# Fewer waits of VectorE on its own semaphore in the attention stage of a transformer block on eight cores

## The chip, the cores and the metric

The kernel runs on all 8 cores of one Trainium2 chip. Each core works on its own 2 of the 16 sequences and sends nothing to the others. The metric is the device time in microseconds (us) of the slowest core; lower is better. The profile is of one execution, on the slowest of its cores (core 3).

## The reference

One pre-norm block: windowed causal attention, then a feed-forward part with ternary weights and 8-bit activations. x is 16 x 2048 x 1024, float32, with 16 heads of 64 and a window of 128.

```python
qkv = layernorm(x) @ w_qkv                 # q, k, v: 16 heads of 64
scores = q k^T / 8, kept where (j <= i) & (j > i - 128)
x = x + (softmax(scores) v) @ w_out
h = gelu(bitlinear(layernorm(x), W1, b1))  # 1024 -> 4096
x = x + bitlinear(h, W2, b2)               # 4096 -> 1024
# bitlinear: weights rounded to -1, 0, 1 times mean|W|,
# activations rounded to 8 bits by the token's absolute maximum
```

## The kernel before, in words

A core has 4096 tokens, cut into 32 tiles of 128 tokens. The program has two stages. The attention stage goes over the 32 tiles, writes each tile's x + attention to a scratch tensor in HBM, and on the side prepares the ternary weights. The feed-forward stage then goes over the 32 tiles again. The change touches only the attention stage.

The order of the work is written out by hand. Each call of `op(engine, fn, waits, nosync=...)` appends one instruction to a list; at the end `mk` (line 1257) walks over the list once per engine. Three rules of it matter:

- Every VectorE (DVE), ScalarE (ACT) and GpSimd instruction raises its engine's own semaphore by one: sV for VectorE, sA for ScalarE. TensorE (PE) raises sP at the end of a group.
- The semaphores named in `waits` are waited for with one `wait_ge` each (line 1268), unless the engine has already waited for as high a value.
- Unless the instruction has `nosync=True`, one more `wait_ge` is put before it (line 1273), on the engine's own semaphore at the number of instructions issued so far. The engine then waits until its previous instruction has completed. Below this is called the own wait.

```python
for (s, val) in waits:
    if val > 0 and lastw.get(s.name, 0) < val:
        eng.wait_ge(s.h, val)
        lastw[s.name] = val
...
if zs is not None and zi > 0 and not ns:
    eng.wait_ge(zs.h, zi)
inst = fn(eng)
```

In the attention stage a tile t is worked on with parts of tile t+1 between. On VectorE, in order:

- `a_ln1_stats(t+1)`: sum over the tile's x (L493), then three instructions on one column (L496, L499, L502). L493 needs the transfer of x, which is issued after L798 of the tile before.
- For each of four groups g of four heads: `a_sm_max`, two maxima over half a group's scores each (L656, L661), which need TensorE's scores; ScalarE's exponentials (L683) follow; `a_sm_norm`, a reciprocal of two row sums (L700), two scalings of 128x256 (L713), another reciprocal (L708), two more scalings. The scaled probabilities are transposed by TensorE (L734), copied by ScalarE (L745), and multiplied with v (L763).
- `a_ln2_fin(t-1)`: L821, L825, L828 on one column.
- `a_ln1_apply(t+1)`: L518 on one column; ScalarE then writes the normalized x (L523), TensorE transposes it (L534), ScalarE copies it (L540).
- Weight preparation, eight tasks to a tile. Tiles 0 to 15 do absolute sums (L402, L409); tiles 16 to 31 round a piece of weights (L421, L426, L430), which TensorE transposes (L443) and VectorE copies out (L455 or L464). I call them sum tiles and rounding tiles.
- From the start of TensorE's q projection of tile t+1 (L556 into psA): the last group's scaling, the k copy (L574), the copy of the attention output (L776), the residual add (`a_res`, L798), and the v copy (L580). Here TensorE does the q, k and v projections (L556 into psA, psB, psC) and the output projection (L787).

TensorE takes the work in program order: scores of group 0 and 1; scores of group 2, transposes and product of group 0; scores of group 3, those of group 1; the transposes of x; those of group 2; then the q projection.

Of the kernel before, what the change touches and what calls it, by code (L numbers as in the profile page):

```python
# [43 lines left out]
def _build(nt, mode="full", cut=None):  # L44
# [106 lines left out]
    with ExitStack() as ctx:  # L151
# [6 lines left out]
        sP = _Sem("sP"); sV = _Sem("sV"); sA = _Sem("sA"); sG = _Sem("sG")  # L158
        dX = _Sem("dX"); dS = _Sem("dS"); dL = _Sem("dL"); dO = _Sem("dO")
# [11 lines left out]
        def op(ek, fn, waits=(), inc=None, amt=1, is_dma=False,  # L171
               nosync=False):
            if fn is not None and not is_dma and ek in _ES:
                inc = _ES[ek]
                amt = 1
            OPS.append((ek, [w for w in waits if w is not None and w[1] > 0],
                        fn, inc, amt, is_dma, nosync))
            if inc is not None:
                inc.n += amt
                return inc.n  # L180
            return None
# [6 lines left out]
        ms = {}  # L188
# [35 lines left out]
        def _memset(ap_, val):  # L224
# [21 lines left out]
                waits=[(dY, _w)], inc=sA)  # L246
        _b = dma("act", bbf_d[0:HF].rearrange("(p k) -> p k", p=128), bstage_bf,
                 dY, waits=[(sA, _a)])
        dma("act", b1bf, bbf_d[0:HF].rearrange("(a k) -> a k", a=1), dY,
            waits=[(dY, _b)])  # L250
        _w = dma("act", bstage[:, 0:8], b2_d.rearrange("(p k) -> p k", p=128),
                 dY, waits=[(dY, _b)])
        _a = op("act", lambda e: e.activation(out=bstage_bf[:, 0:8],
                                              in_=bstage[:, 0:8], func=AF.Copy),
                waits=[(dY, _w)], inc=sA)
# [3 lines left out]
            waits=[(dY, _b)])  # L259
        ms["bias_ld"] = dY.n  # L260

        xin_ld = {}
# [39 lines left out]
        if mode == "S":  # L302
            v = op("dve", lambda e: e.tensor_copy(out=outbuf, in_=wqkv_sb[:, 0:D]),
                   waits=[(sV, wc_v), (sA, wc_a), (dX, dX.n), (dY, ms["bias_ld"]),
                          (dC, ms["consts_ld"])])
# [180 lines left out]
        def a_ln1_stats(t):  # L486
            par = t % 2
            cl = cells[t % 2]
            va = op("act", lambda e, x=xin[par], c=cl: e.activation(
                out=outbuf, in_=x, func=AF.Square,  # L490
                accum_out=c[:, CEL_SSQ:CEL_SSQ + 1]),
                waits=[(dX, xin_ld[t])], inc=sA)
            op("dve", lambda e, x=xin[par], c=cl: e.tensor_reduce(  # L493
                out=c[:, CEL_SUM:CEL_SUM + 1], in_=x, axis=AX.X, op=ALU.add),
                waits=[(dX, xin_ld[t])])
            op("dve", lambda e, c=cl: e.tensor_scalar(  # L496
                out=c[:, CEL_M:CEL_M + 1], in0=c[:, CEL_SUM:CEL_SUM + 1],
                scalar1=1.0 / D, scalar2=None, op0=ALU.mult))
            op("dve", lambda e, c=cl: e.tensor_tensor(  # L499
                out=c[:, CEL_MSQ:CEL_MSQ + 1], in0=c[:, CEL_M:CEL_M + 1],  # L500
                in1=c[:, CEL_M:CEL_M + 1], op=ALU.mult))
            v = op("dve", lambda e, c=cl: e.scalar_tensor_tensor(  # L502
                out=c[:, CEL_VAR:CEL_VAR + 1], in0=c[:, CEL_SSQ:CEL_SSQ + 1],
                scalar=1.0 / D, in1=c[:, CEL_MSQ:CEL_MSQ + 1],
                op0=ALU.mult, op1=ALU.subtract), waits=[(sA, va)], inc=sV)
            op("act", lambda e, c=cl: e.activation(
                out=c[:, CEL_LNV:CEL_LNV + 1], in_=c[:, CEL_VAR:CEL_VAR + 1],
                func=AF.Ln, bias=c_eps),
                waits=[(sV, v), (sV, ms["memset"])])
            va = op("act", lambda e, c=cl: e.activation(  # L510
                out=c[:, CEL_RSTD:CEL_RSTD + 1], in_=c[:, CEL_LNV:CEL_LNV + 1],
                func=AF.Exp, scale=-0.5), inc=sA)
            ms[("rstd", t)] = va
# [139 lines left out]
        def a_sm_max(t, g):  # L653
            cl = cells[t % 2]
            psX = psA if g % 2 == 0 else psB
            v0 = op("dve", lambda e, p=psX, c=cl, g_=g: e.tensor_reduce(  # L656
                out=c[:, CEL_NMX + 4 * g_:CEL_NMX + 4 * g_ + 2],
                in_=p[:, 0:512].rearrange("p (h k) -> p h k", h=2),
                axis=AX.X, op=ALU.max, negate=True),
                waits=[(sP, ms[("sc_h0", t, g)])], inc=sV)  # L660
            v = op("dve", lambda e, p=psX, c=cl, g_=g: e.tensor_reduce(  # L661
                out=c[:, CEL_NMX + 4 * g_ + 2:CEL_NMX + 4 * g_ + 4],
                in_=p[:, 512:1024].rearrange("p (h k) -> p h k", h=2),
                axis=AX.X, op=ALU.max, negate=True),
                waits=[(sP, ms[("scores", t, g)])], inc=sV, nosync=True)
            ms[("nmx0", t, g)] = v0
            ms[("nmx", t, g)] = v
# [29 lines left out]
        def a_sm_norm(t, g):  # L697
            cl = cells[t % 2]
            ev = ms[("expv", t, g)]
            r0 = op("dve", lambda e, c=cl, g_=g: e.reciprocal(  # L700
                out=c[:, CEL_RCP + 4 * g_:CEL_RCP + 4 * g_ + 2],
                in_=c[:, CEL_SUMS + 4 * g_:CEL_SUMS + 4 * g_ + 2]),
                waits=[(sA, ev[1])], inc=sV)
            rc = r0
            v2 = None
            for hh in range(4):
                if hh == 2:
                    rc = op("dve", lambda e, c=cl, g_=g: e.reciprocal(  # L708
                        out=c[:, CEL_RCP + 4 * g_ + 2:CEL_RCP + 4 * g_ + 4],
                        in_=c[:, CEL_SUMS + 4 * g_ + 2:  # L710
                               CEL_SUMS + 4 * g_ + 4]),
                        waits=[(sA, ev[3])], inc=sV)
                v2 = op("dve", lambda e, c=cl, g_=g, hh_=hh: e.tensor_scalar(  # L713
                    out=probsn[g_ % 2][:, hh_ * 256:(hh_ + 1) * 256],
                    in0=probs[g_ % 2][:, hh_ * 256:(hh_ + 1) * 256],
                    scalar1=c[:, CEL_RCP + 4 * g_ + hh_:
                              CEL_RCP + 4 * g_ + hh_ + 1],
                    scalar2=None, op0=ALU.mult),
                    waits=[(sV, rc)], inc=sV, nosync=(hh in (1, 3)))
                if hh == 1:  # L720
                    ms[("pn0", t, g)] = v2
            ms[("pn", t, g)] = v2
# [73 lines left out]
        def a_res(t):  # L796
            par = t % 2
            v = op("dve", lambda e, x=xin[par], o=x1buf[par]: e.tensor_tensor(  # L798
                out=o, in0=psC, in1=x, op=ALU.add),
                waits=[(sP, ms[("outproj", t)]), (dS, spill_ms.get(t - 2, 0))],  # L800
                inc=sV)
            ms[("res", t)] = v
            psum_free["C"] = (sV, v)
            spill_ms[t] = dma("syncq", x1_d[t * T:(t + 1) * T, :], x1buf[par],
                              dS, waits=[(sV, v)])
# [41 lines left out]
        for t in range(nt):  # L847
# [60 lines left out]
            if t + 2 < nt:  # L908
                xin_ld[t + 2] = dma(
                    "syncq", xin[t % 2], xc[(t + 2) * T:(t + 3) * T, :],  # L910
                    dX, waits=[(sV, ms[("res", t)]), (sA, ms[("xln", t)])])
# [6 lines left out]
        for ek in ("pe", "dve", "act", "pool", "syncq"):  # L918
            waits = [(ENG_SEM[o], a_end[o]) for o in ENG_SEM if o != ek]
# [5 lines left out]
        for j in range(4):  # L925
# [3 lines left out]
                waits=([(dB[0], dB[0].n), (dB[1], dB[1].n)] if j < 2 else [])))  # L929
# [33 lines left out]
        for t in range(min(3, nt)):  # L963
            x1_ld[t] = dma("syncq", x1s(t), x1_d[t * T:(t + 1) * T, :],
                           dL, waits=[(dS, dS.n)])
# [368 lines left out]
```

How the kernel before makes its waits and increments, by code:

```python
        def run(eng):  # L1260
            lastw = {}
            zi = 0
            for (k, waits, fn, inc, amt, is_dma, ns) in OPS:
                if k != ek:
                    continue
                for (s, val) in waits:
                    if val > 0 and lastw.get(s.name, 0) < val:
                        eng.wait_ge(s.h, val)
                        lastw[s.name] = val
                if fn is None:
                    continue
                if zs is not None and zi > 0 and not ns:
                    eng.wait_ge(zs.h, zi)
                inst = fn(eng)
                if zs is not None and not is_dma:
                    zi += 1
                if inc is not None:
                    inst.then_inc(inc.h, amt)
```

## Time and profile before

| | us |
|---|---|
| median of 2 runs | 3181.88 (3154.82 and 3208.95) |
| the profiled execution, its time | 3148.21 |
| its span on core 3 | 3146.6 |
| the spans of all cores | 3135.2 to 3146.6 |
| VectorE busy in that span | 2002.7 |
| TensorE busy in that span | 2248.0 |

The time of an execution is 1.6 us more than the span of its slowest core; what lies outside the span is small. All eight cores have the same work, and their spans lie within 12 us.

### The profile page before, as it was taken

What the parts mean: (1) busy time and instruction counts of PE and PEld (TensorE: products, weight loads), DVE (VectorE), ACT (ScalarE), POOL (GpSimd) and SP (SyncE); (2) the same over time, 40 slices, a digit from 0 to 9 for tenths busy, and PEclk for the clock granted to TensorE, in tenths of its full rate; (3) what the DMA queues carried; (4) which work ended last, traced back from release to release, by engine and by line L of the source; (5) the groups of instructions that cost most, each with busy time, mean ns of one, the idle gap of its engine ahead of it and who ended that gap; (6) DMA issues with size and microseconds to landing.
All of it is one profiled execution on the core that took longest, in us unless ns stands there. A gap on an engine that the chain in (4) does not pass through costs nothing.

```text
span 3146.6 us, 41087 instructions; the slowest of 8 cores (3135.2 to 3146.6 us)
## 1 busy us (share of the span) xinstructions
PE 2248.0 (71%) x13196; PEld 1077.6 (34%) x13196; DVE 2002.7 (64%) x3711; ACT 1066.6 (34%) x2064; POOL 17.8 (1%) x36
## 2 busy tenths in 40 slices
PE   0376676676666666666666588888888888888887
PEld 0133333333333333333333233333333333333332
DVE  1245545545546566666666577778777778777775
ACT  1345545544534344444343122222222222222221
POOL 0000000000000000000000000000000000000000
PEclk9977786787777777777776899999999999999998
DMA  4222122222211111122322300000000000000000
GB/s 156 91 76 73 61 74 68 64 71 68 72 51 59 58 61 61 64 81 74 88 74 68 137 27 28 27 15 27 27 27 27 28 14 28 27 27 27 27 15 20
DMA packets 94344, 170.69 MB, mean 54 GB/s; under 512 B 41138, under 2 KB 41394, under 8 KB 93619
## 3 DMA queue, kind: packets, MB, share of 16 engines
q1 hardware_dynamic: 84480, 125.86, 13.0%
q10 hardware_dynamic: 5044, 25.44, 2.3%
q0 software_dynamic: 4608, 16.78, 1.3%
q8 instruction: 108, 1.77, 0.2%
q14 instruction: 104, 0.85, 0.1%
HBM read 126.09 MB, written 41.95 MB: 53 GB/s over the span
## 4 chain that ended last, share of the span: by engine, by line
PE 55%; DVE 17%; ACT 11%; issue 9%; DMA 6%; DVEq 1%; ACTq 0%; SPq 0%; POOLq 0%
PE psC L1191 15%; PE psA L983 8%; PE psB L983 7%; PE psA L556 5%; ACT hqT L1174 4%; PE psC L787 4%; PE psB L556 4%; DMA xin<-xc 3%; DVE probs L713 2%; DVE cells L661 2%; DVE wqch L430 2%; ACT probsT L745 2%; DMA wstgB<-wqkv 2%; PE psC L556 1%; ACT qT L609 1%
## 5 line engine op out<-in xcount | busy, mean ns | idle before, releaser
L1191 PE MATMUL psC<-W2qT,hqT 128*128 128x512 bf16 x2048 | 489.6, 391 | 121.7 <-ACT hqT L1174 121.7
L1191 PEld LDWEIGHTS psC<-W2qT,hqT 128*128 128x128 bf16 x2048 | 192.3, 99 | 368.8 <-issue 173.7
L983 PE MATMUL psA<-W1qT,xqT 128*128 128x512 bf16 x1024 | 249.0, 387 | 0.0
L983 PE MATMUL psB<-W1qT,xqT 128*128 128x512 bf16 x1024 | 243.2, 380 | 0.0
L1007 DVE TENSOR_REDUCE cells<-h_sb 128x1 f32<-128x1024 f32 x128 | 150.2, 1212 | 143.2 <-ACT h_sb L1000 143.2
L763 PE MATMUL psC<-probsT,v_hist 128*64 128x128 bf16 x1024 | 75.1, 289 | 204.3 <-ACT probsT L745 204.3
L955 DVE TENSOR_TENSOR tib<-t1a,tfb 128x1024 f32<-128x1024 f32 x160 | 196.0, 1225 | 17.0 <-DVE tfb L954 0.5
L574 DVE CAST k_sb<-psB 128x1024 bf16<-128x1024 f32 x32 | 39.2, 1224 | 233.6 <-PE psB L556 233.6
L1174 ACT ACTIVATE hqT<-psD 128x1024 bf16<-128x1024 bf16 x64 | 65.5, 1024 | 330.2 <-PE psD L1164 330.2
L1174 ACT ACTIVATE hqT<-psF 128x1024 bf16<-128x1024 bf16 x64 | 65.5, 1024 | 325.8 <-PE psF L1164 325.8
L556 PE MATMUL psA<-wqkv_sb,xlnT 128*128 128x512 bf16 x512 | 174.3, 516 | 1.4 <-ACT xlnT L540 1.4
L957 DVE SCALAR_TENSOR_TENSOR hq<-tfb,tib 128x1024 bf16<-128x1024 f32 x128 | 156.8, 1225 | 13.7 <-DVE tib L955 0.5
L631 PE MATMUL psA<-kT_hist,qT 64*128 64x128 bf16 x512 | 63.4, 260 | 129.2 <-ACT probs L683 128.0
L713 DVE TENSOR_SCALAR probs<-probs,cells 128x256 bf16<-128x256 bf16 x512 | 123.4, 283 | 46.1 <-DVE cells L700 23.4
L556 PE MATMUL psC<-wqkv_sb,xlnT 128*128 128x512 bf16 x512 | 115.6, 379 | 50.3 <-DVE x1b L798 50.3
L798 DVE TENSOR_TENSOR x1b<-psC,xin 128x1024 f32<-128x1024 f32 x32 | 39.2, 1224 | 150.0 <-PE psC L787 144.4
L983 PEld LDWEIGHTS psA<-W1qT,xqT 128*128 128x128 bf16 x1024 | 90.8, 99 | 124.2 <-issue 35.8
L983 PEld LDWEIGHTS psB<-W1qT,xqT 128*128 128x128 bf16 x1024 | 89.7, 98 | 119.7 <-issue 29.0
L763 PEld LDWEIGHTS psC<-probsT,v_hist 128*64 128x64 bf16 x1024 | 50.6, 146 | 231.8 <-issue 231.8
L683 ACT ACTIVATE probs<-psA,cells 128x256 bf16<-128x256 f32 x256 | 118.0, 473 | 15.9 <-DVE cells L656 12.8
L954 DVE CAST tfb<-tib 128x1024 f32<-128x1024 int32 x160 | 111.0, 694 | 16.8 <-DVE tib L953 0.5
L953 DVE CAST tib<-t1a 128x1024 int32<-128x1024 f32 x160 | 111.0, 694 | 16.5
(159 smaller groups left out, 3733.0 us busy)
## 6 DMA issues: line engine op xcount, KB each, us to landing
wstage<-w SPq DMA_DIRECT2D x256, 256.0 KB, 2.8
xin<-xc SPq DMA_DIRECT2D x32, 512.0 KB, 4.4
x1sp<-x1b SPq DMA_DIRECT2D x32, 512.0 KB, 2.9
y<-outbuf POOLq DMA_DIRECT2D x32, 512.0 KB, 4.6
x1b<-x1sp SPq DMA_DIRECT2D x22, 512.0 KB, 3.8
w2td<-w2st SPq DMA_DIRECT2D x64, 128.0 KB, 2.0
W2qT<-w2td ACTq DMA_DIRECT2D x4, 2048.0 KB, 12.3
wstgA<-wqkv ACTq DMA_DIRECT2D x8, 768.0 KB, 4.6
```

Source lines behind the costliest of these rows:

```text
L556: e.matmul(out=p[:, nn * 512:(nn + 1) * 512], lhsT=xlnT[:, cc * 128:(cc + 1) * 128], rhs=wqkv_sb[:, cc * 3 * D + g * D + nn * 512: cc * 3 ...
L683: e.activation(out=probs[g_ % 2][:, hh_ * 256:(hh_ + 1) * 256], in_=p[:, hh_ * 256:(hh_ + 1) * 256], func=AF.Exp, bias=c[:, CEL_NMX + 4 * ...
L713: v2 = op("dve", lambda e, c=cl, g_=g, hh_=hh: e.tensor_scalar(out=probsn[g_ % 2][:, hh_ * 256:(hh_ + 1) * 256], in0=probs[g_ % 2][:, hh_ ...
L763: kt_=kt, sl=slot, g_=g: e.matmul(out=psC[bp_:bp_ + 64, pp * 128:(pp + 1) * 128], lhsT=v_hist[:, sl * D + h_ * 64: sl * D + h_ * 64 + 64], ...
L787: pv = op("pe", lambda e, cc=c, nn=n: e.matmul(out=psC[:, nn * 512:(nn + 1) * 512], lhsT=attnout[:, cc * 128:(cc + 1) * 128], rhs=wout_sb[ ...
L953: op("dve", lambda e: e.tensor_copy(out=tib, in_=t1b))
L955: op("dve", lambda e: e.tensor_tensor(out=cbb, in0=t1b, in1=tfb, op=ALU.is_ge))
L957: rl = op("dve", lambda e, rr=r, d=dst_ap: e.scalar_tensor_tensor(out=d[:, rr * 1024:(rr + 1) * 1024], in0=tfb, scalar=-641.0, in1=cbb, op ...
L983: e.matmul(out=p[:, nn * 512:(nn + 1) * 512], lhsT=xqT[:, cc * 128:(cc + 1) * 128], rhs=W1qT[:, cc * HF + jj * 1024 + nn * 512: cc * HF + ...
L1007: op("dve", lambda e, jj=j, c=cl: e.tensor_reduce(out=c[:, FH + jj:FH + jj + 1], in_=h_sb[:, jj * 1024:(jj + 1) * 1024], axis=AX.X, op=ALU ...
L1174: evs = op("act", lambda e, rr_=rr, p=sp: e.activation(out=hqT[:, rr_ * 1024:(rr_ + 1) * 1024], in_=p, func=AF.Copy), waits=[(sP, pv)] + ( ...
L1191: pv = op("pe", lambda e, nn=n, kk=k: e.matmul(out=psC[:, nn * 512:(nn + 1) * 512], lhsT=hqT[:, kk * 128:(kk + 1) * 128], rhs=W2qT[:, kk * ...
```

## The change

Six `op` calls of VectorE in the attention stage get `nosync=True` (one of them already had it on two of its four instructions, and now has it on three). No instruction is added, removed or moved; the waits named in `waits` all stay. What goes is the own wait (line 1273) ahead of:

- L493, the sum over x: one in a tile
- L656, the maximum over the first half of a group: four in a tile
- L700 and L708, the two reciprocals: four each in a tile
- L713, the third of the four scalings: four in a tile. It keeps a wait for the same value of sV, since `waits` names the reciprocal just ahead of it
- L798, the residual add: one in a tile

That is 18 in a tile, and 576 in the 32 tiles.

```diff
@@ a_ln1_stats
             op("dve", lambda e, x=xin[par], c=cl: e.tensor_reduce(
                 out=c[:, CEL_SUM:CEL_SUM + 1], in_=x, axis=AX.X, op=ALU.add),
-                waits=[(dX, xin_ld[t])])
+                waits=[(dX, xin_ld[t])], nosync=True)
@@ a_sm_max
-                waits=[(sP, ms[("sc_h0", t, g)])], inc=sV)
+                waits=[(sP, ms[("sc_h0", t, g)])], inc=sV, nosync=True)
@@ a_sm_norm
-                waits=[(sA, ev[1])], inc=sV)
+                waits=[(sA, ev[1])], inc=sV, nosync=True)
...
-                        waits=[(sA, ev[3])], inc=sV)
+                        waits=[(sA, ev[3])], inc=sV, nosync=True)
...
-                    waits=[(sV, rc)], inc=sV, nosync=(hh in (1, 3)))
+                    waits=[(sV, rc)], inc=sV, nosync=(hh > 0))
@@ a_res
                 waits=[(sP, ms[("outproj", t)]), (dS, spill_ms.get(t - 2, 0))],
-                inc=sV)
+                inc=sV, nosync=True)
```

VectorE's rows in a sum tile, from the second group's maximum to the third's, before. In the brackets are the semaphores that an instruction waits for, each named once; cells are the columns of row statistics, probs the probabilities:

```order
L828 SCALAR_TENSOR_TENSOR cells_49<-cells_49 128x1 [waits sV]
L656 TENSOR_REDUCE cells_48<-psB 128x2 [waits sP,sV]
L661 TENSOR_REDUCE cells_48<-psB 128x2 [waits sP]
L700 RECIPROCAL cells_48<-cells_48 128x2 [waits sA,sV]
L713 TENSOR_SCALAR probs_73<-probs_73,cells_48 128x256 [waits sV]
L713 TENSOR_SCALAR probs_73<-probs_73,cells_48 128x256
L708 RECIPROCAL cells_48<-cells_48 128x2 [waits sA,sV]
```

The same rows with the change:

```order
L828 SCALAR_TENSOR_TENSOR cells_49<-cells_49 128x1 [waits sV]
L656 TENSOR_REDUCE cells_48<-psB 128x2 [waits sP]
L661 TENSOR_REDUCE cells_48<-psB 128x2 [waits sP]
L700 RECIPROCAL cells_48<-cells_48 128x2 [waits sA]
L713 TENSOR_SCALAR probs_73<-probs_73,cells_48 128x256 [waits sV]
L713 TENSOR_SCALAR probs_73<-probs_73,cells_48 128x256
L708 RECIPROCAL cells_48<-cells_48 128x2 [waits sA]
```

The order stays. L656, L700 and L708 no longer name sV, and wait only for TensorE or ScalarE.

## Rows read from the trace of the kernel before

**Rows 1.** The head of the page.

```profile
span 3146.6 us, 41087 instructions; the slowest of 8 cores (3135.2 to 3146.6 us)
```

**Rows 2.** Stretches: length; busy us (x instructions) of each engine; clock, DMA share, GB/s.

```profile
141.00:891.00 750.00, 522.54 (x3484) 273.67 (x3484) 379.06 (x958) 369.63 (x847) 0.00 (x0) 0.76 0.21 68
891.00:1740.00 849.00, 556.54 (x3882) 306.57 (x3880) 519.83 (x1218) 361.44 (x839) 0.00 (x0) 0.73 0.22 68
1740.00:3146.00 1406.00, 1153.88 (x5760) 490.45 (x5760) 1081.55 (x1504) 311.46 (x353) 17.62 (x32) 0.97 0.09 31
```

**Rows 3.** The chain that ended last, shares of the whole span.

```profile
PE 55%; DVE 17%; ACT 11%; issue 9%; DMA 6%; DVEq 1%; ACTq 0%; SPq 0%; POOLq 0%
```

**Rows 4.** The chain, 478.2 to 478.7 us: start, us, what (DVEq is VectorE's sequencer).

```profile
478.22 0.02 DVEq L1273
...
478.29 0.18 DVE cells L708
...
478.49 0.02 DVEq L1268
...
478.56 0.02 DVEq L1273
...
478.63 0.09 DVE probs L713
```

**Rows 5.** Timeline of VectorE in a sum tile: start, duration, line.

```profile
478.63 0.48 DVE L713 TENSOR_SCALAR probs<-probs,cells 128x256 bf16<-128x256 bf16 x2 [0.18 <-DVE cells L708]
479.21 0.69 DVE L656 TENSOR_REDUCE cells<-psA 128x2 f32<-128x512 f32 x1
479.82 0.68 DVE L661 TENSOR_REDUCE cells<-psA 128x2 f32<-128x512 f32 x1
```

**Rows 6.** Timeline of VectorE where an unsynced instruction follows a short one.

```profile
902.87 0.16 DVE L383 TENSOR_SCALAR b<-psF 128x1 f32<-128x1 f32 x1
902.98 0.48 DVE L421 TENSOR_SCALAR sgnA<-wstage,b 128x512 bf16<-128x512 f32 x1
```

**Rows 7.** The chain around a residual add (L798).

```profile
460.47 3.58 PE psC L787 x16
...
464.21 0.02 DVEq L1273
...
464.28 1.24 DVE x1b L798
```

**Rows 8.** Timeline of ScalarE and TensorE in the sum tile that begins at 471.88 us.

```profile
474.42 0.20 ACT L510 ACTIVATE cells<-cells 128x1 f32<-128x1 f32 x1
...
474.83 0.47 ACT L683 ACTIVATE probs<-psA,cells 128x256 bf16<-128x256 f32 x1 [0.21 <-DVE cells L656]
...
478.50 0.61 PE L643 MATMUL psA<-masks,identb 128*128 128x256 bf16 x2
...
483.82 1.19 PE L734 MATMUL psF<-identb,probs 128*128 128x128 bf16 x8
...
484.80 1.24 ACT L523 ACTIVATE xln<-xin,cells 128x1024 bf16<-128x1024 f32 x1 [1.70 <-DVE cells L518]
...
485.95 1.00 ACT L745 ACTIVATE probsT<-psF 128x1024 bf16<-128x1024 bf16 x1
...
487.67 1.03 PE L534 MATMUL psD<-identb,xln 128*128 128x128 bf16 x8
...
489.91 0.59 PE L734 MATMUL psF<-identb,probs 128*128 128x128 bf16 x4 [0.34 <-DVE probs L713]
```

**Rows 9.** Timeline of TensorE at the end of a rounding tile's softmax part.

```profile
1030.07 0.58 PE L443 MATMUL psD<-identb,wqch 128*128 128x128 bf16 x4 [0.34 <-DVE wqch L430]
```

**Rows 10.** Who waited for whom, VectorE: us in total, times, longest us.

```profile
DVE cells L493 <- DMA xin<-xc: 8.7, 9, 1.6
```

**Rows 11.** Costliest groups, q and v projections: busy us, mean ns | idle before.

```profile
L556 PE MATMUL psA<-wqkv_sb,xlnT 128*128 128x512 bf16 x512 | 174.3, 516 | 1.4 <-ACT xlnT L540 1.4
L556 PE MATMUL psC<-wqkv_sb,xlnT 128*128 128x512 bf16 x512 | 115.6, 379 | 50.3 <-DVE x1b L798 50.3
```

## The prediction

> **What bounds the kernel now.** The head of the page comes first: 3146.6 us on the slowest of eight like cores [rows 1]. Then the stretches [rows 2]. The attention stage is the first two rows: 750 us for the 16 sum tiles, about 46.9 a tile, and 849 us for the 16 rounding tiles, about 53.1 a tile. The feed-forward stage, 1406 us, holds none of the changed instructions. TensorE's granted clock is 0.76 and 0.73 in the attention rows: it changes between its two levels (1.2 and 2.4 GHz) within a tile. No engine is busy all the time there; VectorE is at 379 of 750 and 520 of 849. The chain gives TensorE 55% and VectorE 17% [rows 3], but over the whole span. So I read one tile in the timeline. It falls in two halves. From L493 to the start of the q projection (about 20 us in a sum tile, more in a rounding tile) VectorE has hardly a gap and TensorE waits for it. From there to the next L493 TensorE is busy and VectorE waits for it. The change can pay only in the first half, and at L798 in the second.
>
> **One own wait.** The chain shows it as the sequencer's step at L1273, which comes only once the scaling has ended; L708 starts 0.07 behind that step (478.22, 478.29) [rows 4]. In the timeline L656 starts 0.10 after the end of the pair ahead of it (478.63 + 0.48 = 479.11, start 479.21), while L661, which has no own wait, starts 0.08 before the end of L656 (479.21 + 0.69 = 479.90, start 479.82) [rows 5]. An own wait therefore costs 0.10 + 0.08, about 0.19 us with rounding. Behind a short instruction of one column it is less: L421 starts 0.05 before the end of L383 [rows 6], so 0.16. That price goes to the L656 of groups 1 and 3 (behind L828 and L518) and in sum tiles to two L700 (behind L409).
>
> At the third scaling two waits stand in a row for one value, L1268 and L1273, 0.07 us apart [rows 4]. The first stays, so only 0.07 goes. At L798 TensorE ends at 464.05 (460.47 + 3.58), and the last of three waits behind it is the one removed (464.21, start 464.28) [rows 7]: again 0.07. The bounds: 0 from a wait that was satisfied long before, 0.19 from a full own wait.
>
> The Trainium skill speaks against all this: its page "VectorE: DVE Perf Modes", section "The DRAIN you can't avoid", says that eight copies took 13.88 us with a semaphore after each and also with one after the last, and that "the semaphore costs nothing extra here". By that rule the sum is 0. The rows above disagree, by 0.19 us a wait; the rule is about raising the semaphore, and here the engine also waits for it.
>
> **What is on the path in a tile.** Up to the end of group 2's scaling there are on VectorE: L493, four L656, three L700, three L708, three third scalings. Group 3's scaling comes behind the start of the q projection, where VectorE has several us to spare; its three cost and save nothing. Without L493 the rest is 10 x 0.19 + 3 x 0.07 = 2.1 us, less 0.06 to 0.12 for the short ones: 2.0.
>
> Not all of it goes through, since the other engines come up. In the sum tile at 471.88 [rows 5, 8]:
>
> - ScalarE's first exponential waits for L656, 0.21 us after L510 ended (474.62, start 474.83). Behind L510 it needs about 0.10 of its own, so it can come only 0.11 earlier, however early L656 is. The scores of group 2 wait for these exponentials, so they come 0.11 earlier too. They end at 479.11 (478.50 + 0.61), and L661 starts at 479.82: slack 0.71. A wait on TensorE needs about 0.11. So L661 can come 0.71 - 0.11 + 0.11 = 0.71 earlier, where VectorE by itself would be 1.0 earlier. Here 0.3 us are lost. I take the same slack for all tiles.
> - Group 1's transposes stand behind the scores of group 3, and these behind group 0's transposes, ScalarE's copy and the product: a chain that moved 0.11. They end at 485.01 (483.82 + 1.19), and would end at 484.90. ScalarE's copy at 485.95 was held by its own queue (L523 to 486.04, which waited for L518). With L518 1.1 us earlier the transposes set it: about 484.98, so 0.97 earlier. The product and the transposes of x follow, which end at 488.70 (487.67 + 1.03) - 0.97 = 487.73.
> - Group 2's transposes come next, 0.59 each half. TensorE had waited 0.34 before the second half, at 489.91. VectorE would let it start about 1.7 earlier (0.71 + 0.16 + 0.19 + 0.07 for group 1, 0.16 for L656, 0.16 + 0.19 + 0.07 for group 2). TensorE is ready at 487.73 + 0.59 = 488.32, which is 1.59 earlier. So the q projection starts 1.6 earlier.
>
> In a rounding tile VectorE also feeds the transposes of the weights, so TensorE is brought back to VectorE's time on the way and at the end ([rows 9]: 0.34 us of waiting for VectorE just before the q projection). Only the 0.3 at the first L661 is lost: 0.71 + 0.45 + 0.16 + 0.45, 1.8 us.
>
> **The sum.**
>
> - 16 sum tiles x 1.6 = 25.6
> - 16 rounding tiles x 1.8 = 28.8
> - L798: 31 x 0.07 = 2.2. TensorE waits for it before the v projection [rows 11], and the transfer of x is issued behind it.
> - L493: 14 rounding tiles x 0.19 = 2.7, and perhaps 0.7 in the sum tiles. In nine tiles of both kinds the transfer of x ends the wait [rows 10], and there it saves nothing; in the other sum tiles I count a tenth of a microsecond.
>
> That makes 60 us: 3148.2 - 60 = 3088 us, 1.9% less. The time is against the profiled execution's own 3148.21; the two runs shown are 0.2% and 1.9% above it, and their median 1.1%.
>
> Late next are L661 of group 2, which will wait 0.3 us for TensorE in each tile, and in the sum tiles TensorE's own queue ahead of group 2's transposes (0.1 us of VectorE's gain is left unused there, and 0.3 before).
>
> **Bounds.** If each own wait saved only the 0.10 of the gap, and none of the overlap, the sum would be near 35 us (10 x 0.10 + 3 x 0.07 = 1.2 a tile, 31 tiles: 37), so 3111. If all of VectorE's 2.0 went through in each tile, with 0.19 for each L493: 32 x 2.0 + 6 + 2 = 72, so 3076. The value between them goes by the rows, which show the overlap in pairs of the same kind. The unknown is TensorE's clock: the q projection's matmuls take 516 ns on average against 379 in psC [rows 11], since the clock comes back within it. That is 16 x 0.137 = 2.2 us a tile, and where in it the clock comes back depends on when the tile began. A shift of 0.4 us in its mean is 13 us over the stage, either way.
>
> **Rivals.**
>
> - *All of it goes through.* For it: VectorE has no gaps in the first half. Against: the 0.71 us of slack at L661, less than the 1.0 saved by then. 3076 us, 2.3% less.
> - *TensorE and ScalarE take more than I count.* At the lower clock they are nearly as late as VectorE in the sum tiles; ScalarE's exponentials, copies and x run one behind another. For it: [rows 8], where TensorE had waited for VectorE only 0.34 us in the end. Half the gain goes through: 3148 - 36 = 3112.
> - *Nothing is saved*, because VectorE's next instruction starts at the same time anyway. Against: [rows 4, 5]. 3148 us. The skill's section named above gives this time.
> - *Slower, by the clock.* If the shifted halves left TensorE at 1.2 GHz through the k projection too, its 16 matmuls would take twice as long: the 16 of L787, at the higher level, take 3.58 us [rows 7]; with some of the time hidden, I put 3.3 us more a tile. In all 31 tiles that is 102, less 60: 3190 us. It decides from 60 / 3.3 = 18 tiles on. Against: before the rise TensorE does the same work as now, and it waits less.
>
> **How the numbers follow.** Chances: forecast 0.58, all of it 0.15, half of it 0.17, nothing 0.06, slower 0.04. The forecast's own range is 3073 to 3103, from the clock's 13 us and 0.1% between runs. The range for 8 in 10 reaches down past the full sum by the clock's luck, to 3060, and up past the half to 3122. 2% (about what a measurement can tell from no change here) is 3085 us. The forecast's case lies below it 4 times in 10 (0.23), the full sum always (0.15): 0.38 faster. Slower by over 2% would need 3211, past my worst case: 0.02. The rest, 0.60, is within 2%.
>
> **What would show it.** Right: VectorE's L656, L700 and L708 start 0.05 to 0.08 before the end of the instruction ahead; L713 behind L708 starts 0.10 after it, where it was 0.17, and behind L700 still 0.17; L661 of group 2 shows a new wait for TensorE (L643) of 0.2 to 0.4 us in most tiles; the sum tiles' stretch of 16 falls from 750 to about 723, the rounding tiles' from 849 to about 815; the feed-forward stage stays at 1406. Wrong: gaps of 0.10 that stay; the q projection starting as late after L493 as before; a mean of L556 into psA far from 516 ns.

## The result and the profile after

The median of the changed kernel is 3092.14 us (11 runs), that of the kernel before 3148.61 (10 runs). The ratio is 0.9806, with a 95% interval from 0.9781 to 0.9831: 1.9% less, about 61 us. The profiled execution took 3082.89 us. The forecast was 3088. In four of the eleven executions cores of one die or of both were granted a lower clock and the time was longer; the median counts them, the ratio doesn't.

The head of the page, two of its costliest groups and its chain of waits, for the changed kernel (core 4, the slowest):

```profile
span 3081.3 us, 40334 instructions; the slowest of 8 cores (3072.8 to 3081.3 us)
...
PE 58%; ACT 13%; DVE 13%; issue 8%; DMA 6%; DVEq 0%; ACTq 0%; SPq 0%; POOLq 0%
...
L556 PE MATMUL psA<-wqkv_sb,xlnT 128*128 128x512 bf16 x481 | 163.7, 514 | 10.0 <-DVE cells L708 5.0
...
L713 DVE TENSOR_SCALAR probs<-probs,cells 128x256 bf16<-128x256 bf16 x512 | 123.7, 283 | 37.7 <-DVE cells L700 23.2
```

In the chain [rows 3] VectorE's share fell from 17 to 13%, its sequencer's from 1 to 0, and ScalarE's rose from 11 to 13%. One thing needs care: the q projection has 481 of its 512 matmuls in the records, one short in each of 31 tiles [rows 11]. The missing one is the first, so the matmul row seems to start 0.4 us late. Below I take the start of the q projection from its first weight load, which is there.

The stretches, cut at the first L493 of tiles 1 and 17 and just behind the last L798. [rows 2] can't be set beside them as it stands: its first cut is 2.6 us behind that L493, its last 6.6 us behind the end of L798. So first the kernel before, cut alike:

```profile
138.44:891.94 753.50, 523.48 (x3494) 274.22 (x3494) 381.58 (x963) 370.22 (x849) 0.00 (x0) 0.76 0.21 68
891.94:1734.00 842.06, 555.60 (x3874) 306.02 (x3871) 518.50 (x1214) 358.85 (x834) 0.00 (x0) 0.73 0.22 67
```

and the changed kernel:

```profile
135.00:855.50 720.50, 510.11 (x3469) 275.91 (x3502) 368.50 (x963) 370.41 (x848) 0.00 (x0) 0.77 0.23 71
855.50:1667.00 811.50, 550.25 (x3831) 308.17 (x3862) 502.38 (x1214) 358.74 (x834) 0.00 (x0) 0.73 0.24 70
1667.00:3081.00 1414.00, 1145.41 (x5648) 490.76 (x5760) 1082.46 (x1508) 313.35 (x359) 17.84 (x32) 0.96 0.10 31
```

Sum tiles: 720.5 where there were 753.5, 33.0 less. Rounding tiles: 811.5 where there were 842.1, 30.6 less. The feed-forward stage is what it was within 2 us (1414 and 1412).

VectorE in the softmax half of a sum tile of the changed kernel (start, duration, line):

```profile
500.92 0.16 DVE L502 SCALAR_TENSOR_TENSOR cells<-cells 128x1 f32<-128x1 f32 x1
501.03 0.69 DVE L656 TENSOR_REDUCE cells<-psA 128x2 f32<-128x512 f32 x1
...
503.46 0.68 DVE L661 TENSOR_REDUCE cells<-psB 128x2 f32<-128x512 f32 x1
504.06 0.15 DVE L700 RECIPROCAL cells<-cells 128x2 f32<-128x2 f32 x1
504.39 0.48 DVE L713 TENSOR_SCALAR probs<-probs,cells 128x256 bf16<-128x256 bf16 x2 [0.17 <-DVE cells L700]
504.79 0.16 DVE L708 RECIPROCAL cells<-cells 128x2 f32<-128x2 f32 x1
505.05 0.48 DVE L713 TENSOR_SCALAR probs<-probs,cells 128x256 bf16<-128x256 bf16 x2
505.45 0.68 DVE L656 TENSOR_REDUCE cells<-psA 128x2 f32<-128x512 f32 x1
506.30 0.69 DVE L661 TENSOR_REDUCE cells<-psA 128x2 f32<-128x512 f32 x1 [0.16 <-PE psA L643]
```

Read the gaps by adding start and duration and looking at the next start. L700 now starts 0.08 before the end of L661; L708 and L656 start 0.08 before the end of L713 (it was 0.10 after, [rows 5]). L713 behind L708 starts 0.10 after it (0.17 before), and behind L700, whose two waits were left, still 0.18. L656 behind the one-column L502 starts 0.05 before its end. And the last row has a new wait: L661 of group 2 for the scores.

The views of L661, what ended the idle time before it; first the kernel before, then the changed one (us in total, times):

```profile
  PE psA L643: 0.3, 1
```

```profile
  PE psA L643: 4.7, 25
```

In 25 of 32 tiles VectorE now waits for group 2's scores, 0.19 us on average. Without a wait L661 starts 0.08 before the end of L656, so a tile that waits loses 0.27.

The chain at a residual add of the changed kernel:

```profile
488.06 3.42 PE psC L787 x15
...
491.50 0.02 DVEq L1268
...
491.57 0.02 DVEq L1268
...
491.63 1.24 DVE x1b L798
```

Of three sequencer steps two are left, and L798 starts 0.15 behind TensorE (488.06 + 3.42 = 491.48), where it was 0.23 in [rows 7]; by the medians over all tiles it is 0.18 and 0.25.

### The profile page after: what moved, and what is told of

Its sections match the earlier page's. It is cut to its first block, busy times and chain, and to the rows that moved or that the text cites. A ratio compares the mean times of both kernels' runs of the same rounds, so it can differ in the third digit from the quotient of the medians.

```text
span 3081.3 us, 40334 instructions; the slowest of 8 cores (3072.8 to 3081.3 us)
## 1 busy us (share of the span) xinstructions
PE 2220.0 (72%) x13019; PEld 1081.5 (35%) x13196; DVE 1973.7 (64%) x3711; ACT 1066.2 (35%) x2064; POOL 18.0 (1%) x36
## 4 chain that ended last, share of the span: by engine, by line
PE 58%; ACT 13%; DVE 13%; issue 8%; DMA 6%; DVEq 0%; ACTq 0%; SPq 0%; POOLq 0%
PE psC L1191 15%; PE psA L983 8%; PE psB L983 7%; PE psA L556 5%; ACT hqT L1174 4%; PE psB L556 4%; PE psC L787 4%; DMA xin<-xc 3%; ACT probsT L745 3%; DVE wqch L430 2%; ACT probs L683 2%; DMA wstgB<-wqkv 2%; PE psC L556 2%; ACT qT L609 1%; PE psA L975 1%
## 5 line engine op out<-in xcount | busy, mean ns | idle before, releaser
L1191 PE MATMUL psC<-W2qT,hqT 128*128 128x512 bf16 x1984 | 471.4, 384 | 128.0 <-ACT hqT L1174 125.4
L983 PE MATMUL psA<-W1qT,xqT 128*128 128x512 bf16 x992 | 257.7, 403 | 3.3 <-issue 2.5
L556 PE MATMUL psA<-wqkv_sb,xlnT 128*128 128x512 bf16 x481 | 163.7, 514 | 10.0 <-DVE cells L708 5.0
L713 DVE TENSOR_SCALAR probs<-probs,cells 128x256 bf16<-128x256 bf16 x512 | 123.7, 283 | 37.7 <-DVE cells L700 23.2
L798 DVE TENSOR_TENSOR x1b<-psC,xin 128x1024 f32<-128x1024 f32 x32 | 39.2, 1225 | 149.6 <-PE psC L787 149.6
```

Of the source, the lines that this page charges most:

```text
L556: e.matmul(out=p[:, nn * 512:(nn + 1) * 512], lhsT=xlnT[:, cc * 128:(cc + 1) * 128], rhs=wqkv_sb[:, cc * 3 * D + g * D + nn * 512: cc * 3 ...
L983: e.matmul(out=p[:, nn * 512:(nn + 1) * 512], lhsT=xqT[:, cc * 128:(cc + 1) * 128], rhs=W1qT[:, cc * HF + jj * 1024 + nn * 512: cc * HF + ...
L1191: pv = op("pe", lambda e, nn=n, kk=k: e.matmul(out=psC[:, nn * 512:(nn + 1) * 512], lhsT=hqT[:, kk * 128:(kk + 1) * 128], rhs=W2qT[:, kk * ...
```

## The experiments

The whole times of most kernels move by one or two per cent, and so each kernel was also read tile by tile. The table gives means over 14 sum tiles (2 to 15) and 14 rounding tiles (17 to 30), worked out from the timelines of the three engines on the slowest core of each profiled execution: from the v copy (L580) to the start of the q projection (the softmax half), from there to ScalarE's copy of q (L566), and the whole tile from v copy to v copy. The ratio is to the kernel before. The rest of a tile is 18.2 to 18.7 us in all of them.

| kernel | ratio (95%) | sum: softmax half | q | tile | rounding: softmax half | q | tile |
|---|---|---|---|---|---|---|---|
| before | 1 | 22.42 | 5.75 | 46.68 | 29.59 | 5.48 | 53.37 |
| changed | 0.9806 (0.9781 to 0.9831) | 20.53 | 5.63 | 44.48 | 27.40 | 5.82 | 51.42 |
| x1_max_only | 0.9900 (0.9876 to 0.9924) | 21.82 | 5.69 | 46.02 | 28.90 | 5.18 | 52.50 |
| x2_norm_only | 0.9827 (0.9801 to 0.9853) | 21.11 | 5.53 | 45.29 | 28.13 | 5.06 | 51.52 |
| x3_ends_only | 0.9963 (0.9942 to 0.9984) | 22.32 | 5.56 | 46.33 | 29.35 | 5.35 | 52.91 |
| x4_more_own_waits | 1.0166 (1.0139 to 1.0194) | 24.40 | 5.55 | 48.46 | 31.58 | 5.07 | 54.92 |
| z1_edits_in_sum_tiles | 0.9771 (0.9745 to 0.9797) | 20.46 | 5.66 | 44.45 | 28.10 | 5.19 | 51.49 |
| y2_sums_behind_maxima | 0.9789 (0.9750 to 0.9828) | 19.70 | 6.41 | 44.43 | 27.42 | 5.61 | 51.23 |
| y3_four_more_waits | 0.9781 (0.9739 to 0.9824) | 20.24 | 5.89 | 44.46 | 27.16 | 5.84 | 51.21 |
| y4_both | 0.9714 (0.9682 to 0.9746) | 19.12 | 5.78 | 43.23 | 27.05 | 5.94 | 51.19 |
| w1_fill_weight_loads | 0.9704 (0.9686 to 0.9723) | 19.06 | 5.62 | 43.00 | 27.15 | 6.07 | 51.43 |
| w2_fill_transposes | 0.9588 (0.9570 to 0.9606) | 18.90 | 4.15 | 41.49 | 26.99 | 5.49 | 50.68 |
| w3_fill_first_gap | 0.9706 (0.9685 to 0.9727) | 19.26 | 5.77 | 43.47 | 27.20 | 5.48 | 50.89 |

### The price of one wait: the edits apart, and more waits

Only the edit at L656:

```diff
@@ a_sm_max, first half
-                waits=[(sP, ms[("sc_h0", t, g)])], inc=sV)
+                waits=[(sP, ms[("sc_h0", t, g)])], inc=sV, nosync=True)
```

> Of the six edits only the one at L656 is made. Theory A (an own wait costs 0.19 us, 0.16 behind a one-column instruction, and VectorE's time passes through until L661 of group 2 meets the scores): 0.19 + 0.16 + 0.19 + 0.16 = 0.70 us a tile, no new wait at L661 of group 2 (its slack falls from 0.71 to about 0.17 above the least possible), 22 us less than before, about 3126. Theory B (only the gap of 0.10 counts): 4 x 0.10, 13 us. Theory C (the semaphore costs nothing and the gain came from a luckier clock): 0 us.

Measured: the softmax half is 0.60 us shorter in sum tiles and 0.69 in rounding tiles (0.72 and 0.62 by the medians of the eight cores), where theory A had 0.70 and B 0.40. The time fell by 1.0%, about 31 us by the ratio and 28 by the medians; the rest of it is in the q projection. Two parts of the 0.70 were priced wrongly, and cancel: the first L656 stands behind L502, 0.16 us long, and starts 0.05 before its end, so it is 0.16 and not 0.19; the last stands behind L518, which also has one column but takes 0.21 us, and starts 0.08 before its end, so it is 0.19 and not 0.16.

Only the edits at L700, L708 and the third L713:

```diff
@@ a_sm_norm
-                waits=[(sA, ev[1])], inc=sV)
+                waits=[(sA, ev[1])], inc=sV, nosync=True)
...
-                        waits=[(sA, ev[3])], inc=sV)
+                        waits=[(sA, ev[3])], inc=sV, nosync=True)
...
-                    waits=[(sV, rc)], inc=sV, nosync=(hh in (1, 3)))
+                    waits=[(sV, rc)], inc=sV, nosync=(hh > 0))
```

> Only the edits at L700, L708 and the third L713 are made. Theory A: three groups on the path, 0.45 us each in rounding tiles and a little less in sum tiles, 1.3 us a tile, 42 us less than before, about 3106, and no new wait at L661 of group 2. Theory B: 3 x (0.10 + 0.10 + 0.07) = 0.8 us a tile, 26 us. Theory C: 0. If A holds, this run and the one with L656 alone add up to 64, while the full change should show about 54 for the same waits, since only together do they meet the new wait at L661.

Measured: 1.31 and 1.46 us less in the softmax half, against 1.29 and 1.35 by theory A and 0.8 by B. The time fell by 1.7%, 54 us by the ratio and 51 by the medians, more than the 42 expected; the q projection became 0.2 and 0.4 us shorter as well.

Only the two at the ends:

```diff
@@ a_ln1_stats
-                waits=[(dX, xin_ld[t])])
+                waits=[(dX, xin_ld[t])], nosync=True)
@@ a_res
-                inc=sV)
+                inc=sV, nosync=True)
```

> Only the edits at L493 and L798 are made. Theory A: 0.07 us at L798 in 31 tiles and 0.19 at L493 where the transfer of x is already there: 4 to 6 us less than before, about 3143. If the full change lived from an earlier transfer of x or an earlier v projection, this run would show 15 us or more.

Measured: 0.10 and 0.24 us less in the half that holds L493, and 0.37% of the time, where 5 us were expected and 12 came by the ratio, 9 by the medians. Neither an earlier transfer nor an earlier v projection carries the change.

The other way round, with own waits added to the kernel before:

```diff
@@ a_sm_max, second half
-                waits=[(sP, ms[("scores", t, g)])], inc=sV, nosync=True)
+                waits=[(sP, ms[("scores", t, g)])], inc=sV)
@@ a_sm_norm, the scalings
-                    waits=[(sV, rc)], inc=sV, nosync=(hh in (1, 3)))
+                    waits=[(sV, rc)], inc=sV, nosync=False)
```

> The kernel before with own waits added where it had none: at L661 (four in a tile) and at the second and fourth L713 (eight in a tile, six of them before the q projection). Theory A: 10 x 0.19 = 1.9 us a tile, all of it on the path since VectorE is what the others wait for, 61 us more than before, about 3209. Theory B: 10 x 0.10, 32 us more, 3180. Theory C: no change. The gaps in the timeline should be 0.10 at each added wait in place of the overlap of 0.08.

Measured: the softmax half is 1.98 us longer in sum tiles and 1.99 in rounding tiles, for 10 waits on the path: 0.20 us each. The timeline of this kernel shows it at L661, which starts 0.11 after the end of L656 where the kernel before has it 0.08 ahead of the end:

```profile
484.62 0.69 DVE L656 TENSOR_REDUCE cells<-psA 128x2 f32<-128x512 f32 x1
485.41 0.69 DVE L661 TENSOR_REDUCE cells<-psA 128x2 f32<-128x512 f32 x1
```

The time rose by 1.66%, 52 us, and not by 61. The softmax halves account for 64; the q projection took 0.2 to 0.4 us less a tile, which gives 10 of it back.

So theory A holds for the softmax half in these kernels, and B and C are out. What no theory of mine had is the column of the q projection: it changes in every kernel, by up to 0.4 us a tile, though nothing touches it. And the parts add up to 3.1% by their ratios, where the whole gives 1.9%.

### Where the missing per cent is

The new wait at L661 explains only some of it. The parts shorten the softmax half by 0.60 + 1.31 + 0.10 = 2.01 us in sum tiles, the whole by 1.89; in rounding tiles by 0.69 + 1.46 + 0.24 = 2.39, the whole by 2.19. That is 5 us over 32 tiles. (The medians of the eight cores put nearly all of it in the sum tiles: 2.17 and 1.86 there, 2.20 and 2.16 in the rounding tiles.) More is in the q projection of the rounding tiles: 0.34 us longer than before with the whole change, and 0.13 to 0.42 shorter with each part. By their whole tiles the parts come to 2.40 and 3.18 us, the whole change to 2.20 and 1.95: 23 us over 32 tiles, 0.7%. The rest of the 1.2% is not in the tiles, and the intervals of the ratios, 0.2 to 0.3% to either side, are wide enough for it. The next kernel takes the gain at L656 and L493 away again, in the rounding tiles alone.

```diff
@@ the changed kernel
-                waits=[(dX, xin_ld[t])], nosync=True)
+                waits=[(dX, xin_ld[t])], nosync=(t <= 16))
...
-                waits=[(sP, ms[("sc_h0", t, g)])], inc=sV, nosync=True)
+                waits=[(sP, ms[("sc_h0", t, g)])], inc=sV, nosync=(t < 16))
```

> The changed kernel, but in the rounding tiles L493 and L656 have their own waits again (the other edits stay everywhere). It tests where 26 us of the parts went, since the three parts alone gave 27, 51 and 9 us and together 61. Theory K (the clock): in the rounding tiles of the changed kernel the q projection takes 5.8 us from its start to ScalarE's copy of q, against 5.1 to 5.4 in the parts, since every tile has the same length of 51.2 us and meets the clock's return at the same point. Here the tile is 0.7 us longer in the first half and at L493, and the q projection falls back to about 5.2: the two cancel, and the time stays that of the changed kernel, 3087 within 5. Theory L (the parts overlap because of the new wait at L661): the q projection stays at 5.8, and the time is 11 us above the changed kernel's, 3098.

Measured: theory K. The softmax half of the rounding tiles is 0.70 us longer than in the changed kernel, the q projection 0.63 shorter, and the tile is the same within 0.1. The ratio is 0.9771, and its interval overlaps the changed kernel's: it isn't slower, and undoing a part of the change cost nothing. The median is 3082.50, where theory K had 3087 within 5 and theory L 3098. How this looks in two neighbouring tiles: the first weight load of the q projection (PEld) and ScalarE's copy that ends it (start, duration), for the changed kernel

```profile
1192.63 0.26 PEld L556 LDWEIGHTS psA<-wqkv_sb,xlnT 128*128 128x128 bf16 x2
1243.80 0.26 PEld L556 LDWEIGHTS psA<-wqkv_sb,xlnT 128*128 128x128 bf16 x2
```

```profile
1198.52 1.02 ACT L566 ACTIVATE q_sb<-psA 128x1024 bf16<-128x1024 f32 x1 [7.83 <-PE psA L556]
1249.70 1.02 ACT L566 ACTIVATE q_sb<-psA 128x1024 bf16<-128x1024 f32 x1 [7.85 <-PE psA L556]
```

and for the one with the edits undone in these tiles:

```profile
1196.96 0.25 PEld L556 LDWEIGHTS psA<-wqkv_sb,xlnT 128*128 128x128 bf16 x2
1248.07 0.25 PEld L556 LDWEIGHTS psA<-wqkv_sb,xlnT 128*128 128x128 bf16 x2
```

```profile
1202.14 1.02 ACT L566 ACTIVATE q_sb<-psA 128x1024 bf16<-128x1024 f32 x1 [7.12 <-PE psA L556]
1253.29 1.02 ACT L566 ACTIVATE q_sb<-psA 128x1024 bf16<-128x1024 f32 x1 [7.17 <-PE psA L556]
```

5.89 and 5.90 us in the first, 5.18 and 5.22 in the second, and from one copy to the next 51.18 and 51.15. The first of each pair of q projections, cut where the granted clock (the third number from the right) rises; changed kernel, then the other:

```profile
1192.63:1196.80 4.17, 3.95 (x12) 1.63 (x12) 3.25 (x11) 0.00 (x0) 0.00 (x0) 0.50 0.24 64
1196.80:1198.52 1.72, 1.72 (x13) 0.90 (x12) 1.34 (x3) 0.00 (x0) 0.00 (x0) 1.00 0.50 148
```

```profile
1196.96:1199.70 2.74, 2.74 (x10) 1.06 (x9) 2.04 (x9) 0.00 (x0) 0.00 (x0) 0.50 0.26 88
1199.70:1202.14 2.44, 2.44 (x17) 1.26 (x16) 2.12 (x5) 0.00 (x1) 0.00 (x0) 1.00 0.35 105
```

The q projection begins at 1.2 GHz (0.50) and ends at 2.4 (1.00), with 4.17 us at the lower level in the first and 2.74 in the second. Half of the difference is 0.72 us, the difference of 5.89 and 5.18. It is so everywhere: in 356 of the 364 tiles behind the table the projection takes 3.78 us, which is its time when all of it runs at 2.4 GHz, and half of the time that it spent at the lower level, within 0.05 us. When the rise comes is not tied to the projection's start, and an earlier start only means more matmuls at the lower level.

### The cap in the sum tiles

The changed kernel, with the sum over x behind the first group's maxima in the sum tiles:

```diff
@@ the tile loop, tiles 0 to 15
-            a_ln1_stats(t + 1)
+            a_ln1_sq(t + 1)      # ScalarE's square (L489), as before
             a_scores(t, 0)
             a_sm_max(t, 0)
+            a_ln1_dve(t + 1)     # L493, L496, L499, L502
             a_sm_exp(t, 0)
...
             a_sm_exp(t, 1)
+            a_ln1_rstd(t + 1)    # L506, L510
```

> The changed kernel, but in sum tiles L493 to L502 come behind the first group's two maxima, and ScalarE's two one-column steps behind the second group's exponentials. So the first exponentials no longer stand behind the sum over x and its transfer. If the chain from L493 over the first exponentials and the scores of group 2 is what caps the gain: L661 of group 2 waits for nothing any more (0.3 us), the waits for the transfer of x in 7 of 14 sum tiles are gone (1.1 us each), the transposes of x come earlier (0.15 us); 1 us a sum tile, 17 us less than the changed kernel, 3071. If the cap lies elsewhere: only the transfer's waits go, 8 us, 3079. The clock may add or take 10 us.

Measured: both waits are all but gone. In the sum tiles VectorE waits once for scores at the second maximum (0.4 us) and once for the transfer of x (0.7), where it was 14 times and 7 times (2.8 and 6.5 us in all). VectorE's timeline in this kernel (its L672, L677 and L504 are L656, L661 and L493 of the others) begins the maxima before the v copy's record ends, and L677 of group 2 follows without a gap:

```profile
494.86 1.23 DVE L596 CAST v_hist<-psC 128x1024 bf16<-128x1024 f32 x1 [3.87 <-PE psC L572]
496.00 0.68 DVE L672 TENSOR_REDUCE cells<-psA 128x2 f32<-128x512 f32 x1
496.60 0.68 DVE L677 TENSOR_REDUCE cells<-psA 128x2 f32<-128x512 f32 x1
497.19 1.21 DVE L504 TENSOR_REDUCE cells<-xin 128x1 f32<-128x1024 f32 x1
...
502.33 0.68 DVE L672 TENSOR_REDUCE cells<-psA 128x2 f32<-128x512 f32 x1
502.93 0.68 DVE L677 TENSOR_REDUCE cells<-psA 128x2 f32<-128x512 f32 x1
```

The softmax half of the sum tiles is 0.83 us shorter, of the 1.0 expected. But the q projection is 0.78 longer, and the tile is 44.43 against 44.48. The whole gain went back to the clock; of the 17 us expected, the tiles of both kinds together leave 4. The ratio's interval (0.9750 to 0.9828) doesn't part it from the changed kernel.

More of the same kind of edit:

```diff
@@ the changed kernel: L518, the first L713, the absolute sums
-                waits=[(sA, ms[("rstd", t)])], inc=sV)
+                waits=[(sA, ms[("rstd", t)])], inc=sV, nosync=True)
...
-                    waits=[(sV, rc)], inc=sV, nosync=(hh > 0))
+                    waits=[(sV, rc)], inc=sV, nosync=True)
...
-                    out=accw[:, 4:5], in_=s, axis=AX.X, op=ALU.add,
+                    out=accw[:, k:k + 1], in_=s, axis=AX.X, op=ALU.add,
...
-                           pst["acc_rd"]], nosync=True)
+                           pst["acc_rd2"]], nosync=True)
```

> The changed kernel with more of the same: no own wait at L518, nor at the first L713 (its named wait for the reciprocal stays), and the absolute sums write two columns in turn, so that the second L402 of a pair doesn't wait for L409. On VectorE before the q projection: 0.16 to 0.19 for L518, 3 x 0.07, and 2 x 0.16 in sum tiles. Theory A with the cap: rounding tiles gain 0.40 us, sum tiles 0.3 of 0.7: 11 us less than the changed kernel, 3076. Without the cap 18 us, 3069. The clock may add or take 10 us.

Measured: the softmax half fell by 0.29 us in sum tiles, as expected with the cap, and by 0.24 in rounding tiles, where 0.40 were expected. In sum tiles 0.26 of it went to the q projection, and the tile stayed at 44.46. The median, 3076.19, is the forecast's, but the interval (0.9739 to 0.9824) leaves the size open.

Both together, the reorder of the sum tiles and the waits of the last diff:

```diff
@@ the tile loop, tiles 0 to 15
-            a_ln1_stats(t + 1)
+            a_ln1_sq(t + 1)
...
+            a_ln1_dve(t + 1)
...
+            a_ln1_rstd(t + 1)
@@ the absolute sums as in the last diff; L518, and the first L713
-                waits=[(sA, ms[("rstd", t)])], inc=sV)
+                waits=[(sA, ms[("rstd", t)])], inc=sV, nosync=True)
...
-                    waits=[(sV, rc)], inc=sV, nosync=(hh > 0))
+                    waits=[(sV, rc)], inc=sV, nosync=True)
```

> Both of the last two together. If the cap in sum tiles is gone with the sums behind the maxima, all of the 0.7 us on VectorE counts there: 17 + 11 + 6 = 34 us less than the changed kernel, 3053. If it isn't, 17 + 11 = 28 at most, 3059. The clock may add or take 10 us.

Measured: 0.9714, about 29 us below the changed kernel by the ratios, where 34 or 28 were expected; the tiles of the table give 24. The softmax half of the sum tiles is 1.41 us shorter than in the changed kernel, and here the tile went down with it, to 43.23. The rounding tiles stayed at 51.19.

### The clock itself

If the clock takes what VectorE gives, the next step is to keep TensorE's clock up in the softmax half. Three kernels on top of the last one put work of no use into TensorE's idle time:

```diff
@@ the tile loop; w1: 40, 10, 14, 10; w2: 32, 8, 14, 6; w3: 32, 0, 0, 0
+            fill(n0)
             a_scores(t, 2)
...
             a_pt(t, 0)
+            fill(n1)
...
             a_pt(t, 1)
+            fill(n2)
...
             a_pt(t, 2)
+            fill(n3)
@@ fill in w1
+                op("pe", lambda e: e.ldweights(identb))
@@ fill in w2 and w3; p is the buffer that the next transposes overwrite
+                op("pe", lambda e, p=p: e.transpose(
+                    out=p[:, 0:128], in_=identb, identity=identb),
+                    waits=([psum_free[k], (dC, ms["consts_ld"])]
+                           if i == 0 else []))
```

> The fastest version so far (sums behind the maxima, four more waits gone; 3056) with weight loads of the identity put into TensorE's idle time before the q projection: 40 ahead of group 2's scores, 10, 14 and 10 behind the transposes of groups 0, 1 and 2. They compute nothing that is used. It asks whether TensorE's own idle time is what sends it to 1.2 GHz in the softmax half. Theory K2 (idle time does it, and weight loads count as work): the q projection takes 3.8 us instead of 5.8, the scores and transposes half their time, 60 us less, about 3000. Theory N (weight loads don't count): the clock stays as it is, and the loads that find no room delay group 2's scores by up to 1 us a tile, 0 to 30 us more.

> The same with transposes of the identity (a full matmul each) into the PSUM buffer that the next real transposes overwrite: 32, 8, 14 and 6. Theory K2: about 3000, with the q projection at 3.8 us. Theory N (the clock falls for another reason than TensorE's idle time): 0 to 30 us more than 3056.

> Only the 32 transposes ahead of group 2's scores, in the one long idle time of TensorE (about 5 us). If that idle time alone sends the clock down: about 3010. If the shorter ones do as well: between 3010 and 3056. If neither: 3056 to 3070.

Measured: the weight loads changed nothing (0.9704; q projection 5.62 and 6.07 us). The 60 transposes brought 0.9588, 4.1% less than before and 1.3% less than without them; the q projection fell to 4.15 us in sum tiles, and in 10 of the 14 it takes 3.78 us, all of it at the higher level. The 32 in the first gap alone brought nothing in sum tiles, and about 0.3 us in rounding tiles. That gap was shorter than the 5 us expected: in y4_both TensorE idles there for 2.4 us in a sum tile and 3.6 in a rounding tile.

One q projection of each, with 32 of the transposes (TensorE) or 40 of the weight loads (PEld) in the first gap of the same tile (start, duration); w2:

```profile
519.50 1.95 PE L863 MATMUL psD<-identb 128*128 128x128 bf16 x32
536.01 3.63 PE L575 MATMUL psA<-wqkv_sb,xlnT 128*128 128x512 bf16 x16
```

and w1:

```profile
531.85 1.66 PEld L192 LDWEIGHTS <-identb 128*128 128x128 bf16 x40
548.47 5.97 PE L575 MATMUL psA<-wqkv_sb,xlnT 128*128 128x512 bf16 x16
```

The stretches of 720 and 805 us of w2 and then of w1; the granted clock is the third number from the right:

```profile
135.00:855.00 720.00, 564.51 (x4750) 335.34 (x4748) 390.35 (x1037) 388.29 (x897) 0.00 (x0) 0.91 0.23 74
855.00:1660.00 805.00, 592.03 (x4652) 354.93 (x4653) 496.20 (x1186) 348.41 (x799) 0.00 (x0) 0.81 0.26 82
```

```profile
135.00:855.00 720.00, 525.17 (x3613) 338.39 (x4858) 379.15 (x1011) 380.88 (x889) 0.00 (x0) 0.79 0.23 72
855.00:1660.00 805.00, 549.54 (x3780) 354.65 (x4900) 487.36 (x1173) 348.45 (x798) 0.00 (x0) 0.73 0.25 75
```

Both have 4,700 to 4,900 weight loads a row; w2 has 1,100 more matmuls in the first row, and the clock is 0.91 against 0.79. The two fillings aren't equally long: the 74 weight loads take 3.6 us of a tile, the 60 transposes 5.2. But the 32 transposes of w3 take only 2.1, and with them the clock is 0.82 and 0.77; the 74 weight loads leave it at 0.79 and 0.73, where y4_both has 0.78 and 0.73. So the difference between the two isn't one of length alone. Theory K2 is right in its mechanism for matmuls and wrong for weight loads. In size it gave 35 of the 60 us: the clock still falls in every tile, in the sum tiles for 3 to 10 us (17 to 20 in y4_both) and mostly back before the q projection, in the rounding tiles for 14 to 24 us, and there no q projection runs wholly at 2.4 GHz.

## Why the prediction was right

**The price of a wait.** Right. 0.19 us was read from gaps of both kinds, and ten added waits gave 0.20 each. The 0.07 for a second wait on the same value and for the one at L798 shows in the gaps (0.18 to 0.11 and 0.25 to 0.18, medians). Two terms were priced wrongly, by 0.03 each and against each other: the L656 of group 0 also stands behind a short instruction (L502), and L518, which was taken for one, isn't as short. The section "The DRAIN you can't avoid" of the page "VectorE: DVE Perf Modes" in the Trainium skill says that the semaphore costs nothing extra; here the two timelines differ by about 0.19 us wherever an engine waits for its own last instruction. That a next instruction which isn't held starts earlier, as the same section says, the trace bears out: without the own wait L656 starts 0.08 before the end of the instruction ahead, with it 0.10 after.

**The path in a tile.** Right in its mechanism, low in its sum. The wait for group 2's scores came as stated, with the first exponentials 0.12 us earlier (0.21 behind the end of L510 before, 0.09 after); with the overlap lost it costs 0.27 us in 25 tiles, where I had 0.3 in all. What failed is a step behind it: that this loss reaches the q projection in the rounding tiles. By the medians of the eight cores the parts take 2.20 us off the softmax half there and the whole 2.16, so nothing is lost; in the sum tiles 0.31 is (2.17 and 1.86), where I had 0.4. The first half, with the wait at L493 taken in, was forecast 1.6 to 1.7 us shorter in sum tiles and 2.0 in rounding tiles, and measured 1.89 and 2.19 on the slowest core. Over 32 tiles that is some 7 us more than forecast.

**The clock.** This was the named unknown of 13 us. In sum tiles the q projection came out 0.12 us shorter, in rounding tiles 0.34 longer, about 3.5 us more over 16 of each. The range held it. But I took it for chance ("where in it the clock comes back depends on when the tile began"), and that is the step that was wrong: it isn't a scatter around a mean. In the changed kernel and in three built on it the rounding tiles are 51.2 to 51.4 us long, and 51.5 in the one with less taken off, while their softmax halves differ by 1.05 us. The sum tiles of four kernels are 44.4 to 44.5, with softmax halves from 19.70 to 20.53. x2_norm_only, with other edits, is at 51.5 too (28.13), and the rounding tiles of x4_more_own_waits are all but the first within 0.3 us of 54.7. In the kernel before and in x1 and x3 the length doesn't settle: neighbouring rounding tiles often differ by 1 to 2 us. So in these kernels a gain was given back until it was large enough to leave such a length; what sets the lengths themselves these runs don't show.

**The rivals.** "All of it goes through" fell at L661 and in the q projection. "Half" (a ratio of 0.989) and "nothing" are outside the interval. "Slower, by the clock" named the right place, TensorE's 1.2 GHz reaching further into the projections, with a much too large price: the k projection stayed at the higher level. The chance of more than 2% less was put at 0.38, and the measured 1.94% with an interval that spans 2% fits that.

**The sum.** 60 us were forecast, about 61 came by the ratio, and 65 between the two profiled executions. Those 65 are 33.0 in the sum tiles, 30.6 in the rounding tiles and 3.4 ahead of them, less 2 behind; of the 3.4, 2.7 us are there before the first edited instruction starts (the first L493, at 113.6 against 116.3), so they don't come from the change. The forecast had stretches shorter by 27 and 34 us. So part of the agreement is luck: the sum tiles gave more than forecast and the rounding tiles less, or, by cause, 7 us more came from the softmax halves and the clock took 3.5 back.

## What to carry to other kernels

Count the waits of an engine on itself: each is about 0.2 us where that engine leads and as good as nothing elsewhere (the three in group 3, behind the start of the q projection, don't show in a tile of x2_norm_only), and they can go wherever the data comes from another engine or from an older instruction. Before adding up such gains, read which span of TensorE's work behind them begins at the lower clock, for it can return every tenth that the other engines save; a test that takes a part of the gain away again shows it. Where TensorE idles in short gaps ahead of a long run of matmuls, matmuls of no use into a PSUM buffer that is overwritten anyway can bring a gain of the same order as the waits: here 1.3% beside their 1.9%.

## What was not expected of the hardware

- The tile's length settles: seven kernels have rounding tiles of 51.2 to 51.5 us, though their softmax halves range from 27.05 to 28.13 us.
- 74 weight loads a tile don't keep the clock up (0.79 and 0.73 granted; 0.78 and 0.73 without them), 60 transposes in the same gaps do (0.91 and 0.81).
- Two waits for the same value, one behind the other, cost 0.07 us more than one, though the second is already satisfied.
- It stays open why the 32 transposes in the longest gap raise the granted clock (to 0.82 and 0.77) and still leave the q projection of the sum tiles at 5.77 us. A run with only the later ones wasn't made.
